# Two more source blocks per tile transposed by TensorE instead of by DMA in layer 2 of a graph attention kernel

## The chip, the cores and the metric

The kernel runs on one core of one Trainium2 chip. The metric is the device time of one execution in microseconds (us). The time before is the median of three runs.

## What is computed

The reference is a two-layer graph attention network over 3125 nodes with 128 features, and a layer norm of the result added to its input:

```python
def transformer_conv(x, src, dst, Wq, bq, Wk, bk, Wv, bv, Ws, bs, H, C, concat):
    q = (x @ Wq + bq).reshape(n, H, C)
    k = (x @ Wk + bk).reshape(n, H, C)
    v = (x @ Wv + bv).reshape(n, H, C)
    alpha = jnp.einsum('ehc,ehc->eh', q[dst], k[src]) / jnp.sqrt(jnp.float32(C))
    amax = jax.ops.segment_max(alpha, dst, num_segments=n)
    p = jnp.exp(alpha - amax[dst])
    denom = jax.ops.segment_sum(p, dst, num_segments=n) + 1e-16
    out = jax.ops.segment_sum(p[:, :, None] * v[src], dst, num_segments=n)
    out = out / denom[:, :, None]
    out = out.reshape(n, H * C) if concat else out.mean(axis=1)
    return out + x @ Ws + bs
...
h = jax.nn.relu(transformer_conv(x, ..., H=4, C=128, concat=True))
out = transformer_conv(h, ..., H=2, C=128, concat=False)
return _layernorm(x + out)
```

There are 103125 edges (50000 in both directions and a loop at each node). Layer 1 has 4 heads, layer 2 has 2.

## The kernel before

The kernel does the attention densely. A first stage builds a 3125 x 3125 mask in DRAM that holds the logarithm of the number of edges from a source to a destination. Then come the attention of layer 1, the projections of layer 2 (`projections2`) and the attention of layer 2, both attentions by the same function `attention`. Destinations are taken in 25 tiles of `TP` = 125 rows, and a tile and a head together are one step, numbered `s`: 100 steps in layer 1, 50 in layer 2.

The 3125 sources are 25 blocks of 128 columns (the last has 53). They are cut into 7 pieces by the table `CUTS`; `EXP_PARTS` and `HALVES` join pieces to larger ranges. In one step:

- **Scores** (`scores`, L1830): TensorE makes a piece of scores from three fp16 products into one of three PSUM banks. VectorE adds the mask and keeps the row maximum (`masked_scores`, L1616), then forms the negative maximum (L1621, L1624).
- **Exponentials** (L1529): ScalarE, in three instructions, over pieces 0 and 1, pieces 2 and 3, and pieces 4 to 6.
- **Two ways to transpose the probabilities.** The sum over the sources needs them with sources on partitions, as a high and a low fp16 part. The first `ND` = 4 pieces (16 blocks, `FB` = 16) go by DMA: ScalarE casts the high part in two halves (`part_hi`, L1538), GpSimd subtracts to get the low part, piece by piece (`low_parts`, L1423), and the SP queue issues four DMA transposes (`flips`, L1353: high half 0, high half 1, low half 0, low half 1) into `prob_flipped`. The last `NQ` = 3 pieces (9 blocks) go by TensorE: fp32 transposes into one of two PSUM banks (`transposes`, L1856), from which ScalarE casts the high part (`high_part`, L1544) and VectorE subtracts for the low part (`low_part`, L1629) into `probT`.
- **Values**: for each block two products, 256 and 128 columns (L1871, L1873), for the pieces that TensorE transposed (`values`) and for those that the DMA did (`flipped_values`).
- **End of a step**: VectorE sums (`value_sum`, L1654 and L1656), GpSimd scales and adds (`finish`, L1431 to L1444). In layer 2 VectorE also takes the row norms (L1721, L1724, L1736).

The order is written out by hand. TensorE goes through seven slots k = 0 to 6 in a step. In slot k it makes the scores of piece (k + 5) mod 7 of a step ahead, and beside it transposes (k = 0, 1, 2), values (k = 2, 3, 4), flipped values of pieces 0, 1, 2 (k = 4, 5, 6) and of piece 3 (k = 0 of the next step). The queries are made at k = 3 (L1819) and the skip product at k = 6 of head 0 (L1842):

```python
n, p = divmod(k + LEAD, NP)
...
    scores(s + n + 1, hn, p)
if k < NQ:
    transposes(s, h, k)
if k == 0 and not (is_first(t) and h == 0):
    flipped_values(s - 1, (h - 1) % H, ND - 1)
if 2 <= k <= NQ + 1:
    values(s, h, k - 2)
if k >= NP - ND + 1:
    flipped_values(s, h, k - (NP - ND + 1))
```

VectorE goes through the same slots: a piece of masked scores, a low part, and at the slots of `CLEAR_AT` it clears a piece of the next mask tile (`clear_mask`, L1602). In layer 2 pieces 0 to 3 are cleared in steps of head 1 at k = 1, 3, 4, 6, and pieces 4 to 6 in steps of head 0 at k = 1, 3, 5. In tiles 13 and 24 VectorE also normalizes finished rows (`NORMS_AT`).

`transposes` waits for all exponentials of its step and for the low part two groups back, which frees its bank; `values` waits for the low part of its group; `flipped_values` waits for the DMA transposes of its half; `scores` waits until the piece that was last in its bank has been masked.

## Time and profile before

| | |
|---|---|
| median of 3 runs | 1841.32 us (1840.94 to 1841.59) |
| the profiled execution | 1843.3 us |
| its span, first to last instruction | 1841.3 us |
| attention of layer 2, from its first query product | 1297.9 to the end |
| busy in the span | PE 95%, DVE 85%, ACT 69%, POOL 64% |
| granted TensorE clock, mean | 0.98 |

The profiler took one execution. PE is TensorE's matmuls, PEld its weight loads, DVE is VectorE, ACT ScalarE, POOL GpSimd, SP the queue that issues the DMAs. A matmul's record is longer than the time for which it holds the engine, since matmuls overlap: from the start of one to the start of the next is what it costs. A row with x3 merges three instructions. In brackets stands the time for which the engine was idle before the row, and what ended it.

### The profile page before, as it was taken

How to read it: one execution, taken by the hardware profiler on the slowest of the kernel's cores; microseconds unless marked ns; L12 is line 12 of the kernel's file. 1: busy time of each engine (PE TensorE's matmuls, PEld its weight loads, DVE VectorE, ACT ScalarE, POOL GpSimd, SP SyncE). 2: the span in 40 equal slices, each digit the busy share in tenths (PEclk: the TensorE clock that was granted, in tenths of full speed). 3: DMA queues.
4: the chain of work that ended last, by engine and by line, in shares of the span. 5: the costliest groups of instructions: out<-in, count | busy, mean ns of one | idle time of the engine just before them, and what ended most of it. 6: DMA issues, size and time to landing. Idle time of an engine off the chain costs nothing. (4 is left out here: it accounts for less than half of the span.)

```text
span 1841.3 us, 45045 instructions
## 1 busy us (share of the span) xinstructions
PE 1742.8 (95%) x15000; PEld 1301.7 (71%) x15000; DVE 1561.1 (85%) x4538; ACT 1262.7 (69%) x2093; POOL 1175.7 (64%) x1464
## 2 busy tenths in 40 slices
PE   3779899999999999999999999989899999999997
PEld 2556567777777777777777777756677777677776
DVE  7999889888888888888888888835798898989896
ACT  4479877777777777777777777732467676667675
POOL 4300056887777776777777777733477777767776
PEclk9799999999999999999999999989899999999999
DMA  6768857776787777778777787582499999989996
GB/s 165 220 189 255 241 129 152 152 155 153 150 163 155 161 153 150 154 159 159 160 153 150 160 158 158 122 233 60 98 172 183 181 180 169 173 175 188 173 184 110
DMA packets 753665, 301.76 MB, mean 164 GB/s; under 512 B 655864, under 2 KB 734076, under 8 KB 750185
## 3 DMA queue, kind: packets, MB, share of 16 engines
q1 hardware_dynamic: 752266, 296.96, 76.9%
q8 instruction: 124, 2.03, 0.5%
q0 software_dynamic: 640, 1.63, 0.3%
q14 instruction: 107, 0.87, 0.2%
q10 hardware_dynamic: 528, 0.26, 0.0%
HBM read 93.63 MB, written 47.83 MB: 77 GB/s over the span
## 5 line engine op out<-in xcount | busy, mean ns | idle before, releaser
L1423 POOL TENSOR_TENSOR prob_parts_l<-prob_l,prob_parts_l 125x512 f16<-125x512 f32 x600 | 720.6, 1232 | 13.4 <-ACT prob_parts_l L1538 13.4
L1529 ACT ACTIVATE prob_l<-prob_l,neg_max_l 125x1024 f32<-125x1024 f32 (+1 forms) x450 | 521.0, 1160 | 6.4 <-DVE neg_max_l L1624 6.1
L1830 PE MATMUL score_l<-room,QT_l 128*128 128x512 f16 (+2 forms) x2100 | 512.2, 353 | 1.4 <-DVE scale_rows L1796 1.2
L1544 ACT CAST probT_l<-transposed_l 128x375 f16<-128x375 f32 x450 | 213.0, 473 | 412.1 <-PE transposed_l L1856 412.1
L1871 PE MATMUL output_l<-V,prob_flipped_l 128*128 128x256 f16 x2400 | 459.9, 273 | 4.1 <-DMA prob_flipped_l<-prob_parts_l 4.1
L1873 PE MATMUL output_l<-V,prob_flipped_l 128*128 128x128 f16 x2400 | 427.9, 219 | 0.0
L1616 DVE CUSTOM_DVE_ANT_0 prob_l<-score_l,mask_even 125x512 f32<-125x512 f32 (+2 forms) x546 | 333.2, 614 | 87.1 <-PE score_l L1830 84.9
L1616 DVE CUSTOM_DVE_ANT_0 prob_l<-score_l,mask_odd 125x512 f32<-125x512 f32 (+2 forms) x504 | 308.2, 613 | 80.9 <-PE score_l L1830 78.7
L1538 ACT CAST prob_parts_l<-prob_l 125x1024 f16<-125x1024 f32 x300 | 309.2, 1032 | 0.1
L1871 PE MATMUL output_l<-V,probT_l 128*128 128x256 f16 x1350 | 272.8, 274 | 3.8 <-DVE probT_l L1629 1.9
L1871 PEld LDWEIGHTS output_l<-V,prob_flipped_l 128*128 128x128 f16 x2400 | 233.8, 97 | 55.5 <-issue 5.4
L1629 DVE TENSOR_TENSOR probT_l<-transposed_l,probT_l 128x375 f16<-128x375 f32 x450 | 244.6, 544 | 22.4 <-ACT probT_l L1544 14.7
L1830 PE MATMUL score_l<-KT,QT_l 128*128 128x512 f16 (+2 forms) x1050 | 257.4, 356 | 3.0 <-DVE piece_max_l L1616 3.0
L1873 PEld LDWEIGHTS output_l<-V,prob_flipped_l 128*128 128x128 f16 x2400 | 234.5, 98 | 28.4
L1830 PEld LDWEIGHTS score_l<-room,QT_l 128*128 128x128 f16 x2100 | 187.3, 98 | 91.3 <-issue 17.3
L1873 PE MATMUL output_l<-V,probT_l 128*128 128x128 f16 x1350 | 247.7, 219 | 0.0
L1411 POOL CAST QT_l<-q_now_l 128x125 f16<-128x125 f32 x150 | 43.6, 290 | 297.1 <-ACT q_now_l L1503 297.1
L1856 PE MATMUL transposed_l<-ident,prob_l 125*128 125x125 f32 (+1 forms) x1350 | 219.8, 271 | 7.4 <-ACT prob_l L1529 6.2
L1856 PEld LDWEIGHTS transposed_l<-ident,prob_l 125*128 125x128 f32 (+1 forms) x1350 | 172.1, 140 | 57.1 <-ACT prob_l L1529 4.0
L1871 PEld LDWEIGHTS output_l<-V,probT_l 128*128 128x128 f16 x1350 | 131.4, 97 | 81.4 <-DVE probT_l L1629 36.4
L1602 DVE SCALAR_TENSOR_TENSOR mask_even<-mask_even 125x512 f32<-125x512 f32 (+2 forms) x168 | 151.1, 899 | 0.0
L1873 PEld LDWEIGHTS output_l<-V,probT_l 128*128 128x128 f16 x1350 | 132.1, 98 | 24.0 <-issue 0.3
(217 smaller groups left out, 2388.4 us busy)
## 6 DMA issues: line engine op xcount, KB each, us to landing
mask_scratch<-log SPq DMA_DIRECT2D x87, 420.0 KB
mask_even<-mask_scratch SPq DMA_DIRECT2D x25, 448.0 KB
mask_odd<-mask_scratch SPq DMA_DIRECT2D x24, 448.0 KB
mask_odd<-mask_scratch SPq DMA_DIRECT2D x12, 896.0 KB
mask_even<-mask_scratch SPq DMA_DIRECT2D x12, 896.0 KB
prob_flipped_l<-prob_parts_l SPq DMA_TRANSPOSE x600, 3.1
hT_scratch<-rowsT_l SPq DMA_DIRECT2D x24, 250.0 KB, 3.5
mask_odd<-mask_scratch SPq DMA_DIRECT2D x12, 471.2 KB
```

Source lines behind the costliest of these rows:

```text
L1411: pool.tensor_copy(QT[:, u, 0, 0:TP], q_now[:, u, :]).then_inc(s_qh, 1)
L1423: pool.tensor_tensor(parts[0:TP, 1, a:b], prob[:, h % 2, a:b], parts[0:TP, 0, a:b], ALU.subtract).then_inc(s_flo, 1)
L1529: act.activation(e, e, ACT.Exp, bias=neg_max[:, h % 2:h % 2 + 1], accum_out=total[:, h % 2, c:c + 1]).then_inc(s_exp, 1)
L1538: act.copy(parts[0:TP, 0, a:b], prob[:, h % 2, a:b]).then_inc(s_fhi, 1)
L1544: act.copy(probT[:, q, 0, 0:n, 0:TP], flipped_in_psum(h, q, n)).then_inc(s_hi, 1)
L1602: dve.scalar_tensor_tensor(piece, piece, STEEP, piece, ALU.mult, ALU.min).then_inc(s_cleared, 1)
L1616: dve.tensor_tensor_reduce(out=prob[:, h % 2, a:b], in0=score_bank(h, p)[0:TP, 0:b - a], in1=mask[parity][:, a:b], scale=1.0, scalar=-3.0e ...
L1629: dve.tensor_tensor(probT[:, q, 1, 0:n, 0:TP], flipped_in_psum(h, q, n), probT[:, q, 0, 0:n, 0:TP], ALU.subtract).then_inc(s_t, 1)
L1830: last = pe.matmul(score_bank(h, p)[:, 0:b - a], QT[:, h % 2, i, :], KT[:, h, j, a:b], start=n == 0, stop=n == len(PRODUCTS) - 1)
L1856: last = pe.transpose(flip_bank(h, q)[0:w, i * TP:(i + 1) * TP], prob[:, h % 2, b * C:b * C + w], ident[0:TP, 0:TP])
L1871: pe.matmul(O[:, 0:2 * C], hi, V[:, b, h, :, :].rearrange("p a c -> p (a c)"), start=start, stop=False, skip_group_check=True)
L1873: return pe.matmul(O[:, 0:C], lo, V[:, b, h, 0, :], start=False, stop=stop, skip_group_check=True)
```

## The change

In layer 2 the DMA transposes 14 of the 25 source blocks instead of 16, and TensorE 11 instead of 9, in groups of 4, 4 and 3 instead of 3, 3 and 3. The pieces of layer 2 are then 512, 512, 384, 384, 512, 512 and 309 columns; they were 512, 512, 512, 512, 384, 384 and 309. The pieces keep their slots, so the ranges of the exponentials become 1024, 768 and 1333 columns (1024, 1024, 1077 before), the halves that go by DMA 1024 and 768 (1024 and 1024), and the mask is cleared and loaded by the new pieces. Layer 1 keeps its table.

```diff
-FB = 16
+DMA_BLOCKS = {1: 16, 2: 14}
 CUTS = ((0, 512), (512, 1024), (1024, 1536), (1536, 2048), (2048, 2432), (2432, 2816), (2816, N))
+CUTS2 = ((0, 512), (512, 1024), (1024, 1408), (1408, 1792), (1792, 2304), (2304, 2816), (2816, N))
...
-FIRST = ((0, CUTS[1][1]), (CUTS[1][1], N))
+FIRST = ((0, CUTS2[1][1]), (CUTS2[1][1], N))
...
-                a, b = FIRST[0][0], CUTS[ND - 1][1]
+                a, b = FIRST[0][0], CUTS2[ND - 1][1]
...
-                            a_p, b_p = CUTS[piece]
+                            a_p, b_p = CUTS2[piece]
...
+    fb, cuts = DMA_BLOCKS[layer], CUTS if layer == 1 else CUTS2
...
-        parts = sb("prob_parts", [C, 2, FB * C], F16)
-        flipped = sb("prob_flipped", [C, 2, 2, FB, C], F16)
-        probT = sb("probT", [C, NQ, 2, 3, C], F16)
+        parts = sb("prob_parts", [C, 2, fb * C], F16)
+        flipped = sb("prob_flipped", [C, 2, 2, fb, C], F16)
+        probT = sb("probT", [C, NQ, 2, max(len(blocks_in(cut)) for cut in cuts[ND:]), C], F16)
...
-                    for i, b in enumerate(blocks_in(CUTS[ND + q])):
+                    for i, b in enumerate(blocks_in(cuts[ND + q])):
                         w = width_of(b)
                         last = pe.transpose(flip_bank(h, q)[0:w, i * TP:(i + 1) * TP], prob[:, h % 2, b * C:b * C + w],
                                             ident[0:TP, 0:TP])
```

Everywhere else in `attention` `CUTS` becomes `cuts` and `FB` becomes `fb`.

**TensorE's order**, at the turn from slot 6 of head 0 to slot 0 of head 1: the skip product, the scores of piece 4 or 5 in the 384s and 512s, the transposes, and the flipped values of piece 3 of the step before. Before:

```order
L1842 MATMUL skip_rows_l<-Ws_sb,h_now_l 125x128 x4
L1830 MATMUL score_l<-KT,QT_l 128x384 x3
L1856 MATMUL transposed_l<-ident,prob_l 128x125 x3
L1871 MATMUL output_l<-V,prob_flipped_l 128x256
L1873 MATMUL output_l<-V,prob_flipped_l 128x128
L1871 MATMUL output_l<-V,prob_flipped_l 128x256
L1873 MATMUL output_l<-V,prob_flipped_l 128x128
L1871 MATMUL output_l<-V,prob_flipped_l 128x256
L1873 MATMUL output_l<-V,prob_flipped_l 128x128
L1871 MATMUL output_l<-V,prob_flipped_l 128x256
L1873 MATMUL output_l<-V,prob_flipped_l 128x128
L1830 MATMUL score_l<-KT,QT_l 128x309 x3
```

The same place in the changed kernel (its lines are numbered 3 higher):

```order
L1845 MATMUL skip_rows_l<-Ws_sb,h_now_l 125x128 x4
L1833 MATMUL score_l<-KT,QT_l 128x512 x3
L1859 MATMUL transposed_l<-ident,prob_l 128x125 x4
L1874 MATMUL output_l<-V,prob_flipped_l 128x256
L1876 MATMUL output_l<-V,prob_flipped_l 128x128
L1874 MATMUL output_l<-V,prob_flipped_l 128x256
L1876 MATMUL output_l<-V,prob_flipped_l 128x128
L1874 MATMUL output_l<-V,prob_flipped_l 128x256
L1876 MATMUL output_l<-V,prob_flipped_l 128x128
L1833 MATMUL score_l<-KT,QT_l 128x309 x3
```

The piece of scores ahead of the transposes is 128 columns wider, a fourth transpose follows the three, and one block of flipped values is gone here (it comes back in `values`).

**VectorE's order** in a step of head 0, slots 1 to 3: low part 1, the clearing of mask piece 4, masked scores, and low part 2. Before:

```order
L1629 TENSOR_TENSOR probT_l<-transposed_l,probT_l 128x3x125
L1602 SCALAR_TENSOR_TENSOR mask_even<-mask_even 125x384
L1636 TENSOR_REDUCE all_total_l<-total_l 125x1
L1616 ISA prob_l,piece_max_l<-score_l,mask_even 125x512
L1616 ISA piece_max_l 125x1
L1629 TENSOR_TENSOR probT_l<-transposed_l,probT_l 128x3x125
```

The same place in the changed kernel:

```order
L1632 TENSOR_TENSOR probT_l<-transposed_l,probT_l 128x4x125
L1605 SCALAR_TENSOR_TENSOR mask_even<-mask_even 125x512
L1639 TENSOR_REDUCE all_total_l<-total_l 125x1
L1619 ISA prob_l,piece_max_l<-score_l,mask_even 125x512
L1619 ISA piece_max_l 125x1
L1632 TENSOR_TENSOR probT_l<-transposed_l,probT_l 128x3x125
```

Nothing changes its place; low part 1 is one block wider and the mask piece cleared between is 128 columns wider.

## Rows read from the trace of the kernel before

**Rows 1.** Busy time of each engine by stretch (its own header line), layer 2's attention.
```profile
core 0: us, PE busy (x) PEld busy (x) DVE busy (x) ACT busy (x) POOL busy (x), PEclk, DMA share, GB/s
1299.72:1319.36 19.64, 16.94 (x93) 9.74 (x94) 13.20 (x45) 9.13 (x16) 7.62 (x11) 0.79 0.41 87
1401.89:1505.10 103.21, 103.21 (x963) 79.64 (x962) 92.39 (x301) 70.63 (x121) 79.20 (x96) 1.00 0.95 179
...
1588.65:1615.62 26.97, 23.14 (x194) 16.57 (x193) 26.29 (x80) 16.54 (x28) 17.50 (x22) 0.94 0.98 181
...
1698.06:1801.39 103.33, 103.32 (x963) 79.67 (x961) 92.66 (x301) 70.62 (x121) 79.17 (x96) 1.00 0.97 179
```
**Rows 2.** Timeline of TensorE, a step of head 0: start us, length us, what.
```profile
1500.73 0.48 PE L1856 MATMUL transposed_l<-ident,prob_l 125*128 125x125 f32 x3
1501.05 0.27 PE L1871 MATMUL output_l<-V,prob_flipped_l 128*128 128x256 f16 x1
...
1504.59 0.28 PE L1871 MATMUL output_l<-V,probT_l 128*128 128x256 f16 x1
...
1505.80 0.81 PE L1830 MATMUL score_l<-KT,QT_l 128*128 128x512 f16 x3
1506.55 0.28 PE L1871 MATMUL output_l<-V,probT_l 128*128 128x256 f16 x1
```
**Rows 3.** Groups by line and shape, 1400 to 1700 us: busy us, mean ns | idle.
```profile
L1423 POOL TENSOR_TENSOR prob_parts_l<-prob_l,prob_parts_l 125x512 f16<-125x512 f32 x113 | 137.1, 1243 | 0.0
...
L1529 ACT ACTIVATE prob_l<-prob_l,neg_max_l 125x1024 f32<-125x1024 f32 x58 | 66.2, 1144 | 0.5 <-DVE neg_max_l L1624 0.4
L1538 ACT CAST prob_parts_l<-prob_l 125x1024 f16<-125x1024 f32 x57 | 58.8, 1032 | 0.0
...
L1616 DVE CUSTOM_DVE_ANT_0 prob_l<-score_l,mask_odd 125x512 f32<-125x512 f32 x58 | 39.4, 679 | 3.5 <-PE score_l L1830 2.9
...
L1529 ACT ACTIVATE prob_l<-prob_l,neg_max_l 125x1077 f32<-125x1077 f32 x28 | 33.5, 1195 | 0.0
L1856 PEld LDWEIGHTS transposed_l<-ident,prob_l 125*128 125x128 f32 x225 | 29.7, 141 | 9.5 <-DVE probT_l L1629 0.6 <-issue 0.2
...
L1616 DVE CUSTOM_DVE_ANT_0 prob_l<-score_l,mask_odd 125x384 f32<-125x384 f32 x28 | 15.3, 546 | 12.2 <-PE score_l L1830 12.2
```
**Rows 4.** Timeline of VectorE, the same step and the next.
```profile
1500.42 1.42 DVE L1602 SCALAR_TENSOR_TENSOR mask_even<-mask_even 125x512 f32<-125x512 f32 x1
...
1503.99 0.54 DVE L1629 TENSOR_TENSOR probT_l<-transposed_l,probT_l 128x375 f16<-128x375 f32 x1
1504.44 0.92 DVE L1602 SCALAR_TENSOR_TENSOR mask_even<-mask_even 125x384 f32<-125x384 f32 x1
...
1505.95 0.54 DVE L1629 TENSOR_TENSOR probT_l<-transposed_l,probT_l 128x375 f16<-128x375 f32 x1
```
**Rows 5.** Timeline of VectorE in the step of head 1 that follows.
```profile
1511.97 0.56 DVE L1616 CUSTOM_DVE_ANT_0 prob_l<-score_l,mask_even 125x384 f32<-125x384 f32 x1 [1.33 <-PE score_l L1830]
...
1515.04 0.68 DVE L1602 SCALAR_TENSOR_TENSOR mask_odd<-mask_odd 125x512 f32<-125x512 f32 x1
```
**Rows 6.** Timeline of TensorE in layer 2's first step.
```profile
1313.99 0.54 PE L1856 MATMUL transposed_l<-ident,prob_l 125*128 125x125 f32 x3 [2.70 <-ACT prob_l L1529]
...
1314.79 0.83 PE L1856 MATMUL transposed_l<-ident,prob_l 125*128 125x125 f32 x3
1315.42 1.49 PE L1830 MATMUL score_l<-KT,QT_l 128*128 128x512 f16 x3
```
**Rows 7.** TensorE in tile 13, and the clock of its five microseconds (view of stretches).
```profile
1611.34 1.14 PE L1830 MATMUL score_l<-KT,QT_l 128*128 128x512 f16 x3 [2.72 <-DVE piece_max_l L1616]
...
1610.00:1615.00 5.00, 3.66 (x15) 2.25 (x16) 4.90 (x17) 1.86 (x4) 2.21 (x4) 0.67 0.88 195
```
**Rows 8.** Timeline of TensorE, the one wait for a DMA transpose in mid-layer.
```profile
1539.57 0.27 PE L1871 MATMUL output_l<-V,prob_flipped_l 128*128 128x256 f16 x1 [1.01 <-DMA prob_flipped_l<-prob_parts_l]
```
**Rows 9.** Timeline of TensorE in the last two steps.
```profile
1827.14 0.51 PE L1856 MATMUL transposed_l<-ident,prob_l 125*128 125x125 f32 x3 [1.58 <-ACT prob_l L1529]
...
1832.41 0.27 PE L1871 MATMUL output_l<-V,prob_flipped_l 128*128 128x256 f16 x1
1833.07 0.27 PE L1871 MATMUL output_l<-V,prob_flipped_l 128*128 128x256 f16 x1 [0.33 <-DMA prob_flipped_l<-prob_parts_l]
```

More of the change, by code:

```diff
@@ L1291, in attention @@
         PART_PIECES = ((0, 1), (2, 3), (4, 5), (6,)) if layer == 1 else ((0, 1, 2, 3), (4, 5, 6))
-        MASK_PARTS = [(CUTS[pieces[0]][0], CUTS[pieces[-1]][1]) for pieces in PART_PIECES]
+        MASK_PARTS = [(cuts[pieces[0]][0], cuts[pieces[-1]][1]) for pieces in PART_PIECES]
         CLEAR_AT = ({(0, 2): 0, (0, 5): 1, (1, 2): 2, (1, 5): 3, (2, 1): 4, (2, 4): 5, (2, 6): 6} if layer == 1 else
@@ L1417, in low_parts @@
                     for p in range(ND):
-                        a, b = CUTS[p]
+                        a, b = cuts[p]
                         half = half_of(p)
@@ L1540, in high_part @@
                 def high_part(s, h, q):
-                    n = len(blocks_in(CUTS[ND + q]))
+                    n = len(blocks_in(cuts[ND + q]))
                     act.wait_ge(s_tp, NQ * s + q + 1)
@@ L1596, in clear_mask @@
                 def clear_mask(t, p):
-                    a, b = CUTS[p]
+                    a, b = cuts[p]
                     j = next(j for j, pieces in enumerate(PART_PIECES) if p in pieces)
@@ L1604, in masked_scores @@
                 def masked_scores(s, h, p, parity):
-                    a, b = CUTS[p]
+                    a, b = cuts[p]
                     if h == 0:
@@ L1626, in low_part @@
                 def low_part(s, h, q):
-                    n = len(blocks_in(CUTS[ND + q]))
+                    n = len(blocks_in(cuts[ND + q]))
                     dve.wait_ge(s_hi, NQ * s + q + 1)
@@ L1825, in scores @@
                         pe.wait_ge(s_q, s + 1)
-                    a, b = CUTS[p]
+                    a, b = cuts[p]
                     wait(pe, s_masked, NP * s + p + 1 - score_bank_back(h, p))
@@ L1878, in values @@
                         wait(pe, s_sum, s)
-                    for i, b in enumerate(blocks_in(CUTS[ND + q])):
+                    for i, b in enumerate(blocks_in(cuts[ND + q])):
                         hi, lo = (probT[:, q, n, i, :] for n in range(2))
@@ L1887, in flipped_values @@
                         pe.wait_ge(s_flip[half][n], 16 * (s + 1))
-                    for b in blocks_in(CUTS[p]):
+                    for b in blocks_in(cuts[p]):
                         hi, lo = (flipped[:, h % 2, n, b, :] for n in range(2))
-                        last = product(h, b, hi, lo, stop=b == FB - 1)
+                        last = product(h, b, hi, lo, stop=b == fb - 1)
                     last.then_inc(s_fv, 1)
```

4 lines of the change are left out of this document (2 added, 2 removed).

## The prediction

> **What bounds the kernel now.** I read the busy time by stretch first, since the change touches only the attention of layer 2, then TensorE's timeline, then the other engines where TensorE meets them. In the middle of layer 2 TensorE is the bound without a gap: in five tiles from 1401.89 us it is busy 103.21 of 103.21 us, and in five tiles from 1698.06 us 103.32 of 103.33 [rows 1]. So a tile (two steps) takes 20.64 us, and that is TensorE's own work. VectorE is busy 92.4 of those 103.2 us, GpSimd 79.2, ScalarE 70.6. The DMA engines' share is 0.95 to 0.97, so they look nearly full, but TensorE does not wait for them in either stretch; outside the tail it waits for a DMA transpose once, for 1.01 us [rows 8]. TensorE loses time in three places: the first step (16.94 busy of 19.64 us), tile 13, where VectorE also normalizes rows (23.14 of 26.97 us) [rows 1], and the last two steps [rows 9].
>
> **What the change removes.** Per step, two of 16 blocks no longer go by DMA. GpSimd subtracts 256 columns fewer: 1243 ns per 512 [rows 3] makes 0.62 us less. ScalarE casts 256 columns fewer for the DMA: 1032 ns per 1024 [rows 3] makes 0.26 us. The third and fourth DMA of each part are a quarter smaller. None of this is work on which TensorE waits in mid-layer, so I cost it at nothing there; it counts in the first and last steps, below. Scores and products stay the same in number: pieces of 512, 384 and 309 columns are permuted, and 25 blocks are multiplied in either case.
>
> **What it adds on the path.** Two fp32 transposes per step on TensorE. Three of them hold it from 1500.73 to 1501.05 [rows 2], so one costs 0.107 us, though its record lasts longer (records overlap). A group of four is one more of the same instruction into the same bank (500 of its 512 columns). No row shows a fourth in a group, so I bound it. Below: 0.107. Above: 0.141, the mean weight load [rows 3], if loads no longer hide when four follow one another. I take 0.107, since three in a row already run faster than their loads last. 47 steps (all but the first and the last two) times 2 times 0.107 gives **+10.1 us** (+13.3 at the upper bound).
>
> A rule of the Trainium skill speaks for more: by FP8 and Floating Point Precision, TensorE Precision Notes, true fp32 takes four passes through the array. The trace does not agree for these transposes: 125 columns four times at 2.4 GHz would be 0.208 us, an estimate, where the row shows 0.107. By the rule the term would be +19.6 us.
>
> **The first step.** Its transposes run at the lower clock: three from 1314.79 to 1315.42 are 0.21 us each [rows 6], so two more cost 0.42. They wait for the last exponential (2.70 us of waiting in front of 1313.99 [rows 6]). ScalarE reaches it sooner: the second exponential is 256 columns shorter, the third as much longer (1077 against 1024 columns cost 1195 against 1144 ns [rows 3], 0.96 ns per column, 0.25 us either way), and the second cast is 0.26 shorter. Net **+0.2 us**.
>
> **The last two steps.** No scores are left to cover waits. The transposes of the last step stand after 1.58 us of waiting for ScalarE [rows 9], so their time comes from a chain, not from TensorE's sum. That chain grows in the step before: wider scores in front +0.16 (three times 128 columns at 2.4 GHz), one transpose +0.11, ScalarE's cast of 500 columns instead of 375 +0.12, VectorE's low part +0.13; it shrinks by 0.26 at the cast, 0.25 at one exponential, and grows 0.25 at the other. That is +0.26. In the last step the same three again, +0.36, and 0.33 for the two blocks whose products now stand in `values`, against 0.33 for two pairs of products fewer at the end (0.165 each) and up to 0.49 for the wait for the last DMA transpose (between 1832.41 plus 0.165 and 1833.07 [rows 9]), which comes about 0.9 earlier after a shorter GpSimd chain. Net +0.1, and the bounds are -0.6 and +0.8; I take **+0.1 us**.
>
> **VectorE under TensorE.** Each step it gets two blocks more in its low parts: 128 columns from PSUM cost 679 minus 546 ns [rows 3], so 250 columns cost 0.26 us, 0.52 per tile, where TensorE's tile grows by 0.43. It idles 1.33 us before the masked scores of 1511.97 [rows 5], so it catches up once per tile. Inside the tile the tight spot is low part 2 in steps of head 0. It starts at 1505.95 [rows 4] and lasts 0.54; TensorE starts the products that need it at 1506.55, while its scores before them (three times 0.215 from 1505.80) were done at 1506.44 [rows 2]: it waits 0.1 already. With the change TensorE comes there 0.59 later: 0.21 from the head 1 step before, +0.16 for wider scores, +0.11 and +0.11 for transposes, -0.17 for one flipped block fewer at slot 0, +0.33 for two more blocks of values, -0.16 for narrower scores. VectorE comes there later by 0.13 (wider scores), 0.13 and 0.13 (low parts 0 and 1), 0.13 to 0.5 (mask piece 4 is now 512 columns; 384 took 0.92 here and 512 from 0.68 to 1.42 [rows 4, 5]), and sooner or later by the clearing at the turn of the step, which shrinks from 512 columns and 1.42 us to 384, against masked scores 0.12 longer and 0.38 later in front of it: +0.2. Together +0.6 to +1.0. So the wait lies between none (-0.1 per tile) and 0.25 longer, over 24 tiles -2.4 to +6 us. I take **0**, the value nearest to today's row, but the open side is up.
>
> SBUF — State Buffer, Who interferes with whom, in the Trainium skill says that a VectorE instruction with two SBUF inputs and a GpSimd instruction that reads SBUF exclude each other, and whichever is first blocks the other. The trace agrees in kind: clearing 512 columns takes 1.42 us in one place and 0.68 in another.
>
> **Tile 13.** Here VectorE sets the pace: TensorE waits 2.72 us for masked scores and then runs at a granted clock of 0.67 [rows 7], part of it at the lower level of 1.2 GHz. The two steps take 26.97 us instead of 20.64, 6.3 lost. TensorE's +0.43 is hidden here, VectorE's +0.52 is not, less what a shorter stretch beside GpSimd gives back. I take **0 net** against the +0.43 already counted; bounds -2 (the clock does not fall) and +1.
>
> **Sum:** 10.1 + 0.2 + 0.1 + 0 + 0 = +10.4 us. The profiled execution took 1843.3 us with a span of 1841.3, so it would be 1853.7; the median of the runs shown is 1841.3, and the prediction is against that: **1851.7 us**.
>
> **Rivals.**
> *VectorE becomes the bound of steps of head 0.* For it: 0.52 more per tile against 0.43, a wait of 0.1 that is there today. Against: the idle 1.33 us, and the piece cleared under GpSimd's long instructions is now the narrower one. At 0.25 per tile, +6, it gives 1857.7; twice that 1863.
> *A fourth transpose costs more than the third.* For it: the 141 ns weight loads. At 0.141 it gives 1854.9. Against: three in a row at 0.107. By the page's four passes, worked as twice the row's price (0.214 instead of 0.107), it is 1861.8.
> *Not slower: GpSimd's shorter low parts free VectorE.* In tile 13 VectorE's clearing and normalizing are stretched while GpSimd subtracts. If 0.62 us less per step on GpSimd removes the whole loss of 6.3 us there, with the wait of 1.0 for the DMA, the 0.1 per tile (2.4) and 1.0 of the tail, the gain is 10.7 and the time 1841.0. It decides only if at least 7 of those us go, the point at which the change falls under 0.2%. Against: GpSimd still has 4.4 of its 5.0 us of low parts in each step, and VectorE's work in tile 13 grows.
>
> **How the numbers follow.** The forecast, TensorE's sum with small waits either way (+5 to +14.5), has 0.76; the VectorE rival 0.14; the price of a transpose 0.05; the gain 0.05, of which little goes beyond zero. A measurement can tell about 0.2%, 3.7 us, from no change. So slower 0.93, within it 0.05, faster 0.02. The range takes the low bounds of VectorE's wait and tile 13 at about a third (+6.7) and the VectorE rival's whole price (+16.2): 1848.0 to 1857.5.
>
> **What would show it.** Right: TensorE still 100% busy in five tiles of mid-layer, but those take 105.3 to 105.4 instead of 103.2 us; groups of four transposes hold it 0.43 us; GpSimd's subtractions 0.62 us less per step; DMA share lower, with nothing gained by it. Wrong: waits of TensorE for low parts in most tiles (the first rival), a mid-layer tile at 20.64 or less (transposes hidden, which the full record excludes), or tile 13 at its neighbours' length.

## The result, and the profile after

| | before | after |
|---|---|---|
| median | 1841.45 us (6 runs, 1837.16 to 1845.21) | 1847.76 us (6 runs, 1846.41 to 1848.39) |
| the profiled execution | 1843.3 us, span 1841.3 | 1846.82 us, span 1844.8 |

The ratio is 1.0031, with a 95% interval of 1.0021 to 1.0041: slower by 3.9 to 7.6 us. The prediction was +10.4 us with a range from 1848.0 us, so the direction and the bound were right, the size was too large, and the median lies just under the range.

The busy time of each engine by stretch in the changed kernel, its header first; the lines answer to [rows 1]:

```profile
core 0: us, PE busy (x) PEld busy (x) DVE busy (x) ACT busy (x) POOL busy (x), PEclk, DMA share, GB/s
1298.17:1318.72 20.55, 17.54 (x111) 10.77 (x112) 14.71 (x47) 9.86 (x19) 7.14 (x11) 0.83 0.47 106
1402.48:1507.11 104.63, 104.63 (x982) 82.48 (x981) 92.29 (x301) 70.59 (x121) 74.13 (x96) 1.00 0.87 164
1590.83:1617.15 26.32, 23.56 (x198) 17.05 (x197) 25.93 (x77) 16.79 (x30) 16.00 (x21) 0.94 0.78 168
1700.89:1805.51 104.62, 104.62 (x982) 82.47 (x981) 92.28 (x301) 70.59 (x121) 73.83 (x96) 1.00 0.84 164
```

TensorE is still busy without a gap in mid-layer, but five tiles take 104.63 us instead of 103.21, 0.28 more per tile, where two transposes per step should have given 0.43. The DMA share fell from 0.95 to 0.87 and GpSimd's busy time from 79.2 to 74.1 us, and in these five tiles nothing is seen to come of either (what the relief does give is measured in e5_relief_only). VectorE, which got 2.6 us more of low parts in these five tiles, is not busier than before: 92.29 against 92.39.

TensorE's timeline in the same step as [rows 2]:

```profile
1502.42 0.59 PE L1859 MATMUL transposed_l<-ident,prob_l 125*128 125x125 f32 x4
1502.85 0.27 PE L1874 MATMUL output_l<-V,prob_flipped_l 128*128 128x256 f16 x1
...
1507.81 0.65 PE L1833 MATMUL score_l<-KT,QT_l 128*128 128x384 f16 x3
1508.30 0.27 PE L1874 MATMUL output_l<-V,probT_l 128*128 128x256 f16 x1
```

Four transposes hold TensorE 0.43 us, from 1502.42 to 1502.85: the fourth costs as much as the third. And the wait in front of the third group of values is gone: three scores of 384 columns take 0.49 us and the product follows at once, where before 0.75 lay between the start of three of 512 (0.65) and the product.

VectorE's timeline at the same place: the clear at the turn of the step, the clear of mask piece 4, and low part 2, which these products need; they answer to [rows 4].

```profile
1502.25 0.88 DVE L1605 SCALAR_TENSOR_TENSOR mask_even<-mask_even 125x384 f32<-125x384 f32 x1
...
1506.14 0.68 DVE L1605 SCALAR_TENSOR_TENSOR mask_even<-mask_even 125x512 f32<-125x512 f32 x1
...
1507.41 0.55 DVE L1632 TENSOR_TENSOR probT_l<-transposed_l,probT_l 128x375 f16<-128x375 f32 x1
```

Low part 2 ends at 1507.96 and the product starts at 1508.30, so 0.34 us are to spare where the kernel before waited.

Groups by line and shape, 1400 to 1700 us; they answer to [rows 3]:

```profile
L1426 POOL TENSOR_TENSOR prob_parts_l<-prob_l,prob_parts_l 125x512 f16<-125x512 f32 x56 | 71.3, 1295 | 0.0
L1426 POOL TENSOR_TENSOR prob_parts_l<-prob_l,prob_parts_l 125x384 f16<-125x384 f32 x57 | 55.3, 990 | 0.0
...
L1632 DVE TENSOR_TENSOR probT_l<-transposed_l,probT_l 128x500 f16<-128x500 f32 x57 | 38.5, 675 | 2.1 <-ACT probT_l L1547 2.1
...
L1859 PEld LDWEIGHTS transposed_l<-ident,prob_l 125*128 125x128 f32 x282 | 35.7, 141 | 12.5 <-DVE probT_l L1632 0.7
...
L1605 DVE SCALAR_TENSOR_TENSOR mask_odd<-mask_odd 125x512 f32<-125x512 f32 x29 | 19.8, 683 | 0.0
L1605 DVE SCALAR_TENSOR_TENSOR mask_even<-mask_even 125x512 f32<-125x512 f32 x28 | 19.1, 683 | 0.0
...
L1605 DVE SCALAR_TENSOR_TENSOR mask_odd<-mask_odd 125x384 f32<-125x384 f32 x14 | 11.8, 842 | 0.0
L1605 DVE SCALAR_TENSOR_TENSOR mask_even<-mask_even 125x384 f32<-125x384 f32 x14 | 11.2, 803 | 0.0
```

The same view of the kernel before, for the clearing of the mask, which the rows ahead of the prediction did not show:

```profile
L1602 DVE SCALAR_TENSOR_TENSOR mask_odd<-mask_odd 125x512 f32<-125x512 f32 x28 | 25.0, 892 | 0.0
L1602 DVE SCALAR_TENSOR_TENSOR mask_even<-mask_even 125x512 f32<-125x512 f32 x28 | 24.4, 871 | 0.0
...
L1602 DVE SCALAR_TENSOR_TENSOR mask_odd<-mask_odd 125x384 f32<-125x384 f32 x15 | 11.0, 737 | 0.0
L1602 DVE SCALAR_TENSOR_TENSOR mask_even<-mask_even 125x384 f32<-125x384 f32 x14 | 9.9, 708 | 0.0
```

Clearing 512 columns fell from 880 to 683 ns: in the last slot of head 1, where GpSimd subtracts at the same time, a piece of 384 columns is now cleared, and the wide pieces are cleared at places where it does not subtract. Together these groups went from 70.3 to 61.9 us, 0.6 us per tile less (300 us are some 14 tiles), which pays for the 0.52 us of the wider low parts.

### Where the time went

Each column below is a difference of start times in TensorE's timeline: from layer 2's first query product to the query products of the third step after it (start), then 26 steps, tile 13 (two steps), 18 steps, and from there to the last instruction (end). A pair is two steps in mid-layer, the one that begins between 1480 and 1487 us; most other pairs of the same profile are within 0.03 of it. One profiled execution each.

| kernel | start | 26 steps | tile 13 | 18 steps | end | pair | median us |
|---|---|---|---|---|---|---|---|
| before | 21.51 | 269.29 | 26.97 | 185.77 | 39.86 | 20.64 | 1841.4 |
| the change | 20.55 | 272.11 | 26.32 | 188.36 | 39.26 | 20.92 | 1847.8 |
| e1_old_clear | 18.93 | 273.77 | 26.24 | 189.41 | 39.27 | 21.05 | 1847.7 |
| e2_new_clear_only | 20.09 | 266.63 | 25.11 | 184.56 | 40.11 | 20.52 | 1835.4 |
| e12_new_clear_again | 19.86 | 266.65 | 25.12 | 184.57 | 39.78 | 20.53 | 1835.8 |
| e3_two_extra | 21.47 | 271.46 | 27.07 | 187.99 | 40.22 | 20.87 | 1847.5 |
| e5_relief_only | 19.59 | 267.49 | 24.61 | 185.16 | 38.90 | 20.56 | 1837.7 |
| e6_clear_moved | 19.65 | 268.01 | 27.12 | 185.25 | 39.74 | 20.49 | 1839.9 |
| e7_change_clear_moved | 20.35 | 273.90 | 24.90 | 189.49 | 39.27 | 21.06 | 1848.3 |
| e8_norms_spread | 19.64 | 268.63 | 21.70 | 190.47 | 39.78 | 20.49 | 1840.9 |
| e9_norms_only | 18.19 | 269.36 | 20.86 | 186.55 | 40.07 | 20.64 | 1835.8 |
| e10_clears_and_norms | 19.82 | 266.57 | 20.60 | 186.99 | 39.94 | 20.52 | 1834.1 |
| e11_change_and_norms | 18.01 | 272.14 | 21.78 | 192.67 | 39.26 | 20.92 | 1845.6 |

In the 44 steps outside tile 13 the change costs 2.82 + 2.59 = 5.4 us; 1.1 us of the 269.29 of before are around the one wait for a DMA transpose [rows 8], which the change did not meet, so the steady price is 6.5 us. Tile 13 gave 0.65 back and the end 0.60.

Waits for a DMA transpose come and go between profiles: e9_norms_only has one of 1.07 us, e10_clears_and_norms two (0.30 and 1.13), e6_clear_moved four (0.16 to 0.54) and e8_norms_spread three (0.23 to 0.85), while e2_new_clear_only, e12_new_clear_again and e3_two_extra have none in mid-layer. None of the five kernels that send 14 blocks by DMA has one, which suits a less loaded DMA but does not show it.

The start differs between kernels that do the same there, by 3.3 us between before and e9_norms_only, whose edit acts from tile 13 on, and by 2.5 between the change and e11_change_and_norms. The granted clock goes with it: 0.77 in the 21.51 us of before and 0.91 in the 18.19 of e9_norms_only, 0.83 in the 20.55 of the change and 1.00 in the 18.01 of e11_change_and_norms. So the 0.96 us that the change is shorter there can't be put down to it. It is a part of why the two profiles differ by 3.5 us only: the profiled execution of before is 1.9 us above its median, that of the change 0.9 below its own.

### The profile page after: what moved, and what is told of

Read it like the earlier page. It is cut to its first block and busy times, and to the rows that moved or that the text cites. A ratio compares the mean times of both kernels' runs of the same rounds, so it can differ in the third digit from the quotient of the medians.

```text
span 1844.8 us, 45245 instructions
## 1 busy us (share of the span) xinstructions
PE 1749.2 (95%) x15100; PEld 1313.0 (71%) x15100; DVE 1560.6 (85%) x4538; ACT 1263.1 (68%) x2093; POOL 1152.9 (62%) x1464
## 5 line engine op out<-in xcount | busy, mean ns | idle before, releaser
L1426 POOL TENSOR_TENSOR prob_parts_l<-prob_l,prob_parts_l 125x512 f16<-125x512 f32 (+1 forms) x600 | 700.2, 1199 | 13.3 <-ACT prob_parts_l L1541 13.3
L1532 ACT ACTIVATE prob_l<-prob_l,neg_max_l 125x1024 f32<-125x1024 f32 (+3 forms) x450 | 521.1, 1160 | 7.6 <-DVE neg_max_l L1627 6.4
L1547 ACT CAST probT_l<-transposed_l 128x375 f16<-128x375 f32 (+1 forms) x450 | 223.8, 497 | 414.5 <-PE transposed_l L1859 414.4
L1874 PE MATMUL output_l<-V,prob_flipped_l 128*128 128x256 f16 x2300 | 443.0, 272 | 1.9 <-DMA prob_flipped_l<-prob_parts_l 1.8
L1876 PE MATMUL output_l<-V,prob_flipped_l 128*128 128x128 f16 x2300 | 410.9, 219 | 0.0
L1541 ACT CAST prob_parts_l<-prob_l 125x1024 f16<-125x1024 f32 (+1 forms) x300 | 298.6, 997 | 0.1
L1632 DVE TENSOR_TENSOR probT_l<-transposed_l,probT_l 128x375 f16<-128x375 f32 (+1 forms) x450 | 257.9, 573 | 23.8 <-ACT probT_l L1547 17.8
L1876 PE MATMUL output_l<-V,probT_l 128*128 128x128 f16 x1450 | 263.4, 219 | 0.0
L1874 PEld LDWEIGHTS output_l<-V,prob_flipped_l 128*128 128x128 f16 x2300 | 224.0, 97 | 52.3 <-issue 3.3
L1876 PEld LDWEIGHTS output_l<-V,prob_flipped_l 128*128 128x128 f16 x2300 | 224.6, 98 | 28.4
L1874 PEld LDWEIGHTS output_l<-V,probT_l 128*128 128x128 f16 x1450 | 140.8, 97 | 74.5 <-DVE probT_l L1632 29.8
L1876 PEld LDWEIGHTS output_l<-V,probT_l 128*128 128x128 f16 x1450 | 141.5, 98 | 22.6 <-issue 0.3
```

The source lines that it names most:

```text
L1426: pool.tensor_tensor(parts[0:TP, 1, a:b], prob[:, h % 2, a:b], parts[0:TP, 0, a:b], ALU.subtract).then_inc(s_flo, 1)
L1532: act.activation(e, e, ACT.Exp, bias=neg_max[:, h % 2:h % 2 + 1], accum_out=total[:, h % 2, c:c + 1]).then_inc(s_exp, 1)
L1541: act.copy(parts[0:TP, 0, a:b], prob[:, h % 2, a:b]).then_inc(s_fhi, 1)
L1547: act.copy(probT[:, q, 0, 0:n, 0:TP], flipped_in_psum(h, q, n)).then_inc(s_hi, 1)
L1632: dve.tensor_tensor(probT[:, q, 1, 0:n, 0:TP], flipped_in_psum(h, q, n), probT[:, q, 0, 0:n, 0:TP], ALU.subtract).then_inc(s_t, 1)
L1874: pe.matmul(O[:, 0:2 * C], hi, V[:, b, h, :, :].rearrange("p a c -> p (a c)"), start=start, stop=False, skip_group_check=True)
```

## The experiments

Times in this section are medians of the timed runs; the kernel before was run beside each group, with medians of 1841.34, 1841.11 and 1841.44 us.

### e1_old_clear: the change without its new clears

```diff
-                    a, b = cuts[p]
+                    a, b = CUTS[p]
```

The same in `MASK_PARTS`, the first loads and `projections2`.

> The change, but the mask of layer 2 is still loaded and cleared by the pieces of before (512, 512, 512, 512, 384, 384, 309), which always cover what the scores need. Theory A: the wait of 0.12 us of TensorE in front of the third group of values in steps of head 0 went because VectorE's clearing at that place no longer runs beside a long GpSimd instruction and because wide and narrow clears changed places. Then with the old clears the wait comes back, a pair of steps takes about 21.05 to 21.1 us instead of 20.93, and the kernel is 2.5 to 3.5 us slower than the change. Theory B: it went because TensorE comes to that place later (0.4 to 0.6 us of transposes and values in front of it), whatever VectorE clears. Then a pair stays at 20.93 and the time that of the change within 1 us.

Measured: 1847.73 us, ratio 1.0033 (1.0022 to 1.0045), and a pair of 21.05 us. Neither theory has all of it. The wait in front of the third group of values stayed away, as theory B has it: TensorE comes there later in any case. But the old clears brought another wait, after the third group of transposes in steps of head 0. TensorE's timeline after those transposes:

```profile
1503.35 0.48 PE L1859 MATMUL transposed_l<-ident,prob_l 125*128 125x125 f32 x3
1503.78 0.27 PE L1874 MATMUL output_l<-V,probT_l 128*128 128x256 f16 x1
```

VectorE's, the clear that made it late:

```profile
1500.77 1.14 DVE L1605 SCALAR_TENSOR_TENSOR mask_even<-mask_even 125x512 f32<-125x512 f32 x1
```

Three transposes take 0.32 us, here 0.43 pass until the first product: 0.11 us of waiting in every pair. In the change the piece cleared at that point is 384 columns wide and the products follow at 0.32 (1504.82 to 1505.14). In the profiles this makes 2.7 us in 44 steps (273.77 + 189.41 against 272.11 + 188.36), but the medians of e1 and the change are equal, and I can't say where it comes back. The two ratios, 1.0033 and 1.0031, are each known to some 2 us only, so a gain of 2.7 us from the new clears is neither shown by the times nor excluded by them; the profiles show it in every pair.

### e2_new_clear_only and e12_new_clear_again: the new clears on the kernel before

```diff
-        MASK_PARTS = [(CUTS[pieces[0]][0], CUTS[pieces[-1]][1]) for pieces in PART_PIECES]
+        clear_cuts = CUTS if layer == 1 else CUTS2
+        MASK_PARTS = [(clear_cuts[pieces[0]][0], clear_cuts[pieces[-1]][1]) for pieces in PART_PIECES]
...
-                        dve.wait_ge(s_cleared, NP * (s // H) + p + 1)
+                        dve.wait_ge(s_cleared, NP * (s // H) + p + (2 if layer == 2 and 2 <= p <= 4 else 1))
```

> The kernel before, with 16 blocks by DMA and the old pieces of scores, but the mask of layer 2 loaded and cleared by the new pieces (512, 512, 384, 384, 512, 512, 309). Theory A: the 0.12 us wait goes, a pair of steps takes 20.5 us instead of 20.64, the kernel is about 3 us faster than before. Theory B: no change, 20.64 (or a longer wait, since a wider clear stands in front of low part 2: up to 20.8).

> The kernel before with the clears by the pieces of the change once more. Mid-layer accounts for 2.6 us of gain; its first run gave 6.0. If the rest was chance in tile 13 and at the layer's start (TensorE's granted clock fell there in one profile and not in the other), the gain is now 3 to 5 us; if it is steady, 5.5 to 6.5.

Measured: 1835.35 us, ratio 0.9968 (0.9957 to 0.9980), and again 1835.79, ratio 0.9972 (0.9961 to 0.9983). A pair takes 20.52 us as theory A had it. The second run, 5.2 us faster by the ratio and 5.65 by the medians, lies between its two expectations. TensorE's timeline at the place of the wait:

```profile
1501.27 0.81 PE L1832 MATMUL score_l<-KT,QT_l 128*128 128x512 f16 x3
1502.08 0.22 PE L1875 MATMUL output_l<-V,probT_l 128*128 128x128 f16 x1
```

The wait there is halved, and small ones after the transposes of head 0 are gone, 0.12 us per pair in all. Outside tile 13 the columns give 3.9 us (455.06 to 451.19): 2.6 of it from 22 pairs, 1.1 since the wait for a DMA transpose did not come. Tile 13 gives 1.9 more, alike in both profiles (25.11 and 25.12 us). TensorE still waits there, 2.59 us against the 2.72 of [rows 7], but its clock does not fall: it is 1.00 over the whole tile. TensorE's timeline, then tile 13 in the view of stretches (its columns are those of [rows 1]):

```profile
1605.10 0.81 PE L1832 MATMUL score_l<-KT,QT_l 128*128 128x512 f16 x3 [2.59 <-DVE piece_max_l L1618]
```

```profile
1582.62:1607.73 25.11, 21.54 (x194) 15.60 (x193) 24.87 (x75) 15.56 (x26) 16.98 (x22) 1.00 0.98 177
```

From those scores to the product behind the next ones it takes 2.13 us (1605.10 to 1607.23), where the kernel before took 3.78 at the lower clock (1611.34 to 1615.12). So nearly all of the gain in tile 13 is the clock.

One part of the change, the permuted clears, is thus a gain of 5.2 to 5.9 us by the ratios on the kernel before. In mid-layer it is worth 0.12 us per pair there and 0.13 on top of the transposes (21.05 in e1_old_clear, 20.92 in the change). The rest of it is tile 13, where the clock falls both in the change and in e1_old_clear, and the wait for a DMA transpose, which neither of these two meets.

### e3_two_extra: two transposes more, nothing taken away

```diff
+                    if layer == 2 and q < 2:
+                        last = pe.transpose(flip_bank(h, q)[:, 3 * TP:4 * TP], prob[:, h % 2, b * C:b * C + C], ident[0:TP, 0:TP])
```

> The kernel before with two more fp32 transposes per step of layer 2, a repeated block into the free columns of the bank in the first two groups, whose result nobody reads; nothing is taken from DMA, GpSimd or ScalarE, and VectorE's low parts stay three blocks wide. Each transpose should hold TensorE 0.107 us. Theory A (the wait stays where it was, since VectorE is as before): a pair takes 20.64 plus 0.43, 21.07, and the kernel is 10 us slower than before. Theory B (TensorE comes to the waits later, and they are absorbed): a pair takes 20.9 to 20.95, the kernel 6.5 to 7.5 us slower than before.

Measured: 1847.47 us, ratio 1.0029 (1.0017 to 1.0040), a pair of 20.87: theory B, a little cheaper than it said. TensorE's timeline, the group of three, the added one, and at the place of the wait the scores and the second product of the values' first pair:

```profile
1483.58 0.48 PE L1856 MATMUL transposed_l<-ident,prob_l 125*128 125x125 f32 x3
1483.90 0.27 PE L1859 MATMUL transposed_l<-ident,prob_l 125*128 125x125 f32 x1
...
1508.19 0.81 PE L1830 MATMUL score_l<-KT,QT_l 128*128 128x512 f16 x3
1508.95 0.22 PE L1875 MATMUL output_l<-V,probT_l 128*128 128x128 f16 x1
```

Scores to second product is 0.76 us here, against 0.81 with half a wait in e2_new_clear_only. Of the 0.43 us that four transposes add to a pair, 0.19 fill time in which TensorE waited for VectorE before, and 0.23 lengthen it. VectorE's work was not touched in this kernel, so this is absorption alone. All of the 0.19 is gone here: 0.12 in front of the third group of values and 0.07 after the transposes of head 0. The change's pair is 0.05 us longer than this one: that is VectorE's part in it, a wait of 0.06 after the third transposes of head 1.

### e5_relief_only: 14 blocks by DMA, nothing for TensorE

The products of blocks 14 and 15 take the transposed probabilities of blocks 12 and 13, so part of the sum is left out.

```diff
+                        at = b - 2 if layer == 2 and b >= 14 else b
-                        hi, lo = (flipped[:, h % 2, n, b, :] for n in range(2))
+                        hi, lo = (flipped[:, h % 2, n, at, :] for n in range(2))
```

`half_cols` and `low_parts` take 1792 columns in place of 2048 in layer 2.

> The kernel before with only the relief: ScalarE casts, GpSimd subtracts and the DMA transposes 14 blocks in layer 2, while TensorE transposes nine as before and multiplies 25 pairs; the products of source blocks 14 and 15 take blocks 12 and 13 of the transposed probabilities in their place, so that part of the sum is left out. If the relief is worth nothing in mid-layer, as the prediction had it, a pair stays at 20.64 and the kernel is within 1.5 us of before (tile 13 and the last two steps could give about 1 us). If shorter GpSimd work takes away the wait of 0.12 us per pair, 20.5 and 3 to 4 us faster.

Measured: 1837.68 us, ratio 0.9974 (0.9963 to 0.9986). The relief is not worth nothing: 0.08 us per pair, between the two theories, 2.4 in tile 13 (the clock stays at 1.00 there, behind a wait of 2.24 us) and 0.96 at the end. Its runs lie between 1834.51 and 1839.80 us and the profiled one is the lowest, so these columns show the relief at its best; by the medians it is 3.7 us. The end adds up from the two halves: before 39.86, with the relief 38.90, with the extra transposes 40.22; -0.96 and +0.36 make -0.60, and the change has 39.26.

### e6_clear_moved and e7_change_clear_moved: clears of 640, 640, 640, 256, 256, 384 and 309 columns

```diff
+CUTS2 = ((0, 640), (640, 1280), (1280, 1920), (1920, 2176), (2176, 2432), (2432, 2816), (2816, N))
```

> The kernel before, with the mask of layer 2 cleared and loaded by pieces of 640, 640, 640, 256, 256, 384 and 309 columns: little where VectorE's clear runs beside GpSimd (last slot of head 1) or stands in front of low part 2 (slot 1 of head 0), more in the first slots of head 1. With the pieces of the change a wait of 0.06 us was left per pair of steps (20.52 us). Theory: clears at these two places set TensorE's waits, so a pair takes 20.44 to 20.48 us, and the kernel is 1 to 2 us faster than with the clears of the change alone, 6.5 to 8 faster than before. Rival: what is left is not set by the clears, 20.52 and no gain.

> The change (14 blocks by DMA, 11 by TensorE) with the clears of 640, 640, 640, 256, 256, 384 and 309 columns. In the change TensorE has one small wait left per pair, 0.06 us in front of the values after the third transposes of head 1, where no clear stands in front. Theory: the clears are no longer what it waits for, so a pair stays at 20.93 and the kernel within 1.5 us of the change; four transposes per pair, 0.43 us, stay in full. Rival: 20.87 and 1.5 us faster.

Measured: 1839.93 us, ratio 0.9991 (0.9982 to 1.0000), on the kernel before; 1848.31 us, ratio 1.0038 (1.0025 to 1.0052), on the change. Neither theory held. On the kernel before the pair is 20.49 us, as good as with the clears of the change, which is what the rival said. The wait in front of the third group of values is gone, where the clear ahead of low part 2 is 256 columns wide, and the small waits after the transposes of head 0 have stayed. But four of the 22 pairs meet a wait for a DMA transpose and take 0.25 to 0.65 us more, and tile 13 takes 27.12 us with the clock at 0.94, so most of the gain is lost. On the change the pair grew to 21.06, as in e1_old_clear; the time is within 1.5 us of the change, but tile 13 was 1.4 us shorter there, with the clock at 1.00. VectorE's timeline, the clear in the last slot of head 1 (beside GpSimd's subtraction) and the next of the same width:

```profile
1502.77 1.15 DVE L1607 SCALAR_TENSOR_TENSOR mask_even<-mask_even 125x256 f32<-125x256 f32 x1
...
1506.92 0.41 DVE L1607 SCALAR_TENSOR_TENSOR mask_even<-mask_even 125x256 f32<-125x256 f32 x1
```

TensorE's, behind the first of them:

```profile
1505.34 0.48 PE L1861 MATMUL transposed_l<-ident,prob_l 125*128 125x125 f32 x3
...
1505.89 0.22 PE L1878 MATMUL output_l<-V,probT_l 128*128 128x128 f16 x1
```

The record of the pair's first product is missing; the second starts at 1505.89, so the first (0.11 before it) at 1505.78, 0.12 after the three transposes were done (1505.66): the wait of e1 is back, at half the width of the clear. GpSimd's timeline shows why, the two subtractions that meet e7's clears of 1500.62 and of 1502.77:

```profile
1500.78 1.74 POOL L1428 TENSOR_TENSOR prob_parts_l<-prob_l,prob_parts_l 125x512 f16<-125x512 f32 x1
1502.48 1.15 POOL L1428 TENSOR_TENSOR prob_parts_l<-prob_l,prob_parts_l 125x512 f16<-125x512 f32 x1
```

The clear waits until the second subtraction is over (1503.64) and ends 0.28 us behind it; in e1 the clear of 512 columns ends 0.55 behind its subtraction (1501.36 to 1501.91). So the narrow clear did save 0.27 us. But the clear ahead of it is 640 columns wide here, ran first (1500.62 to 1501.50) and held up the subtraction of 1500.78, which took 1.74 us where that of e1, beside 512 columns, took 1.61. Clear, subtraction, subtraction and clear form one chain; what the last clear gained, the wider one ahead of it had lost.

### e8_norms_spread and e9_norms_only: the row norms of tile 13 over six tiles

```diff
-NORMS_AT = {(13, h, k): (6 * h + k - 1,) for h in range(2) for k in range(1, 7)}
+NORMS_AT = {(13 + n // 2, 1, 2 + n % 2): (n,) for n in range(12)}
-STORES_AT = {(14, 0): ((0, 6),), (14, 1): ((6, 12),), (24, 1): ((12, 18),), (NT, 0): ((18, 23), (23, NT))}
+STORES_AT = {(20, 0): ((0, 6),), (20, 1): ((6, 12),), (24, 1): ((12, 18),), (NT, 0): ((18, 23), (23, NT))}
```

> The kernel before with the moved clears (640, 640, 640, 256, 256, 384, 309) and with the twelve row norms of tile 13 spread over tiles 13 to 18, two in each step of head 1 (the first two stores follow at tile 20). Theory: tile 13 is slow because VectorE gets 7 us of norms there, so its pair takes 20.5 instead of 25 to 27, and the kernel is 4 to 6 us faster than with the moved clears alone, some 11 to 13 faster than before. Rival (the loss of tile 13 is only moved): each of the six tiles gets 0.5 to 1 us longer, and at most 1 us is won.

> The kernel before with the twelve row norms of tile 13 spread over tiles 13 to 18 and nothing else. If the loss of tile 13 is VectorE's norms, 5 to 6.3 us faster than before; tiles 13 to 18 at 20.64 to 20.9 us. It also tells how far the time of tile 13 differs between runs of kernels that are alike there.

Measured: with the norms alone 1835.83 us, ratio 0.9972 (0.9962 to 0.9982); with the moved clears beside them 1840.89, ratio 1.0004 (0.9995 to 1.0013). Alone, tile 13 falls from 26.97 to 20.86 us, and each of the later tiles with norms costs only 0.13 more: the theory. The loss of tile 13 [rows 7] is thus VectorE's norms. With the moved clears each of the tiles with norms costs 1.1 us more (its shorter step takes 10.92 to 10.94 us, not 9.82; the 18 steps 190.47, not 185.25), which is what the rival said: the loss has only moved. VectorE's and then TensorE's timeline in such a tile:

```profile
1645.52 1.29 DVE L1604 SCALAR_TENSOR_TENSOR mask_odd<-mask_odd 125x256 f32<-125x256 f32 x1
```

```profile
1647.43 0.81 PE L1832 MATMUL score_l<-KT,QT_l 128*128 128x512 f16 x3 [0.98 <-DVE piece_max_l L1618]
```

A clear of 256 columns falls into GpSimd's subtraction (the clear of 640 columns ahead of it, delayed by a norm, took 1.67 us), and TensorE waits 0.98 us for the masked scores behind it.

### e10_clears_and_norms: the new clears and the spread norms together

The edits of e2_new_clear_only and of e9_norms_only on the kernel before, the main lines:

```diff
+        clear_cuts = CUTS if layer == 1 else CUTS2
...
+NORMS_AT = {(13 + n // 2, 1, 2 + n % 2): (n,) for n in range(12)}
```

> The kernel before with the clears by the pieces of the change (20.52 us per pair in mid-layer against 20.64) and the twelve norms of tile 13 spread over tiles 13 to 18. If the two gains are separate, mid-layer gives 0.12 times 22, 2.6 us, and tile 13 about 5.5: 7 to 9 us faster than before, 1832 to 1834. Rival: both feed on the same slack of VectorE, and the spread norms take back what the clears gave in their six tiles: 5 to 6 us faster, as the norms alone.

Measured: 1834.08 us, ratio 0.9959 (0.9946 to 0.9973), 7.5 us faster than before. It is faster than the kernel before and than the change. Against e2_new_clear_only (0.9968) and e9_norms_only (0.9972) the intervals overlap, so it has the lowest median but is not shown to be the fastest. Mid-layer keeps 20.52 us per pair, tile 13 takes 20.60, and the five tiles after it cost 0.11 more each. 22 us of the stretch with norms:

```profile
1633.00:1655.00 22.00, 22.00 (x205) 17.13 (x204) 20.22 (x68) 14.88 (x27) 16.72 (x21) 1.00 0.98 183
```

TensorE is busy throughout even there. Later it waits twice for a DMA transpose, which lengthens two pairs by 1.7 us together; TensorE's timeline at the longer of the two:

```profile
1751.70 0.27 PE L1873 MATMUL output_l<-V,prob_flipped_l 128*128 128x256 f16 x1 [1.13 <-DMA prob_flipped_l<-prob_parts_l]
```

### e11_change_and_norms: the change without the slow tile

```diff
-NORMS_AT = {(13, h, k): (6 * h + k - 1,) for h in range(2) for k in range(1, 7)}
+NORMS_AT = {(13 + n // 2, 1, 2 + n % 2): (n,) for n in range(12)}
```

> The change with the norms of tile 13 spread in the same way, so that tile 13 hides nothing of what the transposes cost. Against the kernel before with spread norms (1835.8 us) it should cost 0.29 us per pair over 24 pairs, 7 us, less 0.6 in the last two steps: 1842 to 1843. Rival: the clear of tile 13 decided more than that; then the difference is under 5 or over 9 us.

Measured: 1845.60 us, ratio 1.0022 (1.0012 to 1.0032), against 1835.83 for the kernel before with the same norms: 9.8 us by the medians and 9.2 by the ratios (each known to some 2 us), the rival. The columns of the table without the start give 9.0. In the change the tiles with norms take 21.79 us, 0.87 above its 20.92, where the kernel before gave 0.13. VectorE's and then TensorE's timeline in one of them:

```profile
1647.60 1.48 DVE L1605 SCALAR_TENSOR_TENSOR mask_odd<-mask_odd 125x384 f32<-125x384 f32 x1
```

```profile
1652.14 0.81 PE L1833 MATMUL score_l<-KT,QT_l 128*128 128x512 f16 x3 [0.56 <-DVE piece_max_l L1619]
```

The norms push a clear of 384 columns further into GpSimd's subtraction, where it takes 1.48 us; the masked scores behind it come late, and TensorE waits 0.56 us for its bank. So the change did use up slack of VectorE, only not in a way that its own mid-layer tiles show.

## Why the prediction was right or wrong

**The bound, and the cost of a transpose: right.** TensorE is without a gap in mid-layer in either kernel, and the added transposes cost 0.107 us each, four per tile 0.43. The four passes of the Trainium skill (FP8 and Floating Point Precision, TensorE Precision Notes) did not show, here or in e3_two_extra.

**"VectorE under TensorE: I take 0": this is the step that failed.** The wait of 0.1 us was seen and its end was the lower bound, -2.4 us, but I kept today's value. Measured: 0.12 us in front of the third group of values went, and 0.07 in smaller waits after the transposes of head 0, while one of 0.06 came up in head 1 (3 transposes 0.38 us to the product instead of 0.32). That is 0.43 - 0.19 + 0.06, or 0.29 to 0.30 per pair where 0.28 was measured, and 2.9 us less over 44 steps than the 9.4 (44 times 0.214) that the sum gave.

The step had TensorE come to its products 0.59 us later and VectorE to low part 2 0.6 to 1.0 later, so that the wait could only stay or grow. In the traces low part 2 starts 1.46 us later (1505.95 to 1507.41) and TensorE is done with the scores before it 1.86 later (1506.44 to 1508.30), both counted from the start of the profile: TensorE gained 0.40 on VectorE. What was wrong is VectorE's clears. Mask piece 4 was to cost 0.13 to 0.5 more and took 0.24 less (0.92 to 0.68); the clear at the turn of the step took 0.54 less (1.42 to 0.88), and my +0.2 for that place (0.12 and 0.38 later, the clear off) had given it 0.30. The step also knew of one wait only, and not of the 0.07 us after the transposes. Nor are faster clears needed for the waits to go: e3_two_extra leaves VectorE's instructions as they were, and TensorE's own lateness takes away all 0.19. The step's figures were loose as well: VectorE's terms add up to 0.72 to 1.09, and 1.0 against 0.59 would be a wait 0.41 longer, not 0.25.

**The contention: right in kind, used the wrong way.** A clear of 512 columns costs 683 ns alone and 1.42 us beside GpSimd. The rule of the Trainium skill (SBUF — State Buffer, Who interferes with whom) that the first of the two blocks the other fits. It does so in both directions: the clears that fell into a subtraction ended 0.28 to 0.55 us behind it, and a subtraction of 512 columns that fell into a clear ended 1.02 behind that (1501.50 to 1502.52 in e7_change_clear_moved). I used it for the upper bound only, and did not walk through all seven clears by it; the 0.6 us per tile that came back to VectorE lies there.

**Tile 13: "0 net against the +0.43": mis-sized.** Its pair got 0.65 us shorter, where the sum left it 0.43 longer. TensorE's waits of over 0.15 us in it add up to 3.79 us before (0.52, 0.27, 0.28 and 2.72) and to 2.53 in the change (0.27 and 2.26): TensorE waited less for VectorE here too, where the step had VectorE's +0.52 outweigh what it gets back. The relief alone takes 2.4 us off the tile and the clears alone 1.9, but mostly by the clock: in those profiles it stayed at 1.00 over the tile, while in those of before, the change, e1, e3 and e6 it fell, to 0.93 to 0.94 over the tile. In the kernel before, 3.78 us pass from the scores of 1611.34 to the product at 1615.12, where the same stretch takes 2.13 elsewhere (1513.29 to 1515.42): 1.6 us hang on that fall and come or go as a whole. The length of the wait ahead does not decide it: the clock fell behind 2.26 us (the change) and 2.62 (e3_two_extra) and stayed behind 2.24 (e5_relief_only) and 2.59 (e2_new_clear_only, and again e12_new_clear_again). What does stays open. TensorE's wait in the change, behind which the clock falls:

```profile
1612.55 0.90 PE L1833 MATMUL score_l<-KT,QT_l 128*128 128x512 f16 x3 [2.26 <-DVE piece_max_l L1619]
```

**The last two steps: "+0.1": the sign was off.** The column of the end holds one ordinary step besides, so the sum had +0.3 for it; it measured -0.60, which is -0.96 by the shorter ScalarE, GpSimd and DMA chain and +0.36 by the transposes. Up to the transposes of the last step it takes 0.27 us less than before (25.75 us from 1801.39 to 1827.14, now 25.48 from 1805.51 to 1830.99), where I had the chain grow by 0.26; that is most of the error. In the profile after no product waits for a DMA transpose any more, as forecast:

```profile
1830.99 0.62 PE L1859 MATMUL transposed_l<-ident,prob_l 125*128 125x125 f32 x4 [1.30 <-ACT prob_l L1532]
...
1833.80 0.27 PE L1874 MATMUL output_l<-V,probT_l 128*128 128x256 f16 x1 [0.27 <-DVE summed_l L1659]
```

**The first step: not to be told.** +0.2 forecast; the stretch varies by up to 3.3 us with the granted clock between kernels that do the same there.

**GpSimd's saving: too large.** 0.62 us per step forecast, and 4.85 (137.1 us for 28 steps) to 4.5 (126.6) is 0.37: subtracting 384 columns took 990 ns, not 932, and 512 took 1295, not 1243. (And it is the second and the fourth of the step's DMA transposes, those of half 1, that are a quarter smaller.)

Together: 10.4 - 2.9 (waits) - 1.1 (tile 13) - 0.9 (end) is 5.5 us, and the ratio stands for 5.7. That they meet so closely is luck: the wait for a DMA transpose, 1.1 us in the profile of before, is not in this sum, and with it 4.4 would be left, which is in the interval as well. With the prediction's own lower bounds (-2.4 for VectorE's wait, -2 for tile 13, -0.7 for the end) the sum would be +5.3, close to what was measured; its range took the one for tile 13 at a third only. Of the rivals, the one that had GpSimd's and VectorE's relief give time back described what happened, at half its size and in part through another cause (TensorE's lateness); the one that made VectorE the bound came up only in the tiles with norms of e11_change_and_norms.

## What to carry to other kernels

When work is added to the engine that bounds, subtract the small waits that stand behind the place where it is added: a line busy without a gap still hid 0.19 us of waits in a pair of 20.64. When the sizes of a table are permuted, walk through every use of the table, not only the one that the change is about: here clearing the mask by the new sizes was worth 5.2 to 5.9 us by itself on the kernel before. Savings of this kind don't add up. By the ratios the relief alone is -4.8 us, the clears alone -5.2 to -5.9 and the transposes alone +5.3, but all together, with VectorE's wider low parts (not run alone), +5.7. In a mid-layer pair one sees why: the transposes fill 0.19 us of waits, the clears take 0.12 and the relief 0.08 of the same 0.19. So take them apart at once. The lowest median of this study has the old split, the new clears and the norms spread.

## What the runs showed of the hardware

A clear that begins while GpSimd subtracts waits until that subtraction is over, and then takes a rest that depends on its width: it ended 0.28 us behind the subtraction at 256 columns (e6, e7, e8), 0.34 at 309 (before, the change), 0.41 or 0.42 at 384 (the change, e2, e11) and 0.54 or 0.55 at 512 (before, e1). So its whole time depends on when it began as much as on its width: 512 columns took 0.68 us alone and 1.14 or 1.42 beside a subtraction, 384 up to 1.48, 256 0.41 alone and 1.15 to 1.29. The other way round a subtraction of 512 columns that began during a clear ended 1.02 us behind it (before, the change, e1, e7): it takes 1.16 us alone, and took 1.61 beside a clear of 512 columns that ran first and 1.74 beside one of 640. (The profile's spans on GpSimd are rough.)

A fourth fp32 transpose in a row costs 0.107 us like the third, though the weight loads' records average 141 ns.

Two kernels with the same instructions at the start of layer 2 (before and e9_norms_only) differ there by 3.3 us with the granted clock (0.77 and 0.91), more than half of what this change costs. And a wait of TensorE of 2.2 to 2.7 us in tile 13 was followed by a lower clock in some kernels and not in others, which is worth 1.6 us; in the kernel that was run twice (e2 and e12) it stayed both times.
